# Two cross-attentions with refills by the bank, and a last layer whose heads go by pairs

## What is computed

```python
# third block, cross-attention (l2x): 16 query heads and 4 key heads of 128, 128 context rows
q = (h @ Wq + bq).reshape(b, s, 16, 128); k = (ctx @ Wk + bk).reshape(b, se, 4, 128); v = (ctx @ Wv + bv)
q = rmsnorm(q, qn_w); k = rmsnorm(k, kn_w)
x = x + softmax(q @ k.T / sqrt(128) + mask) @ v @ Wo

# fourth block, cross-attention (l3x): self-attention and cross-attention side by side
ln_out = ln(h)                                  # each projection rounds it to fp8 by its own scale
q, k, v = fp8_linear(ln_out, wq | wk | wv);     q, k = ln(q), ln(k)
core = gqa(q, k, v)                             # 64 own keys
qx = ln(fp8_linear(ln_out, wqx));  kx, vx = split(ctx @ w_kv_x);  kx = ln(kx)
xout = gqa(qx, kx, vx)                          # 128 context keys
x = x + fp8_linear(concat(core, xout), wproj)

# fourth block, feed-forward (l3f): latent attention of 16 heads of 16, then 1 + 7 experts of width 128
kv_d, q_d = r @ kv_d_w, r @ q_d_w               # r = rmsnorm(h)
k, q = concat(kv_d @ k_u_w, rope(r @ rope_k_w)), concat(q_d @ q_u_w, rope(q_d @ rope_q_w))
probs = softmax(causal(q @ k.T / sqrt(16)));    out = (probs @ (kv_d @ v_u_w)) @ o_w
h = h + out;  x = x + h + moe(rmsnorm(h))
```

## Time and profile before

| | |
|---|---|
| median of 3 runs | 3697.68 us (3693.32 to 3700.13) |
| the profiled execution | 3693.92 us, span 3692.1 us |
| TensorE busy in the span | 2963.2 us (80%) |
| VectorE | 2257.9 us (61%) |
| ScalarE | 1502.9 us (41%) |
| GpSimd | 585.9 us (16%) |
| first cross-attention of the change (l2x) | 1608.5 to 1956.0 |
| second (l3x) | 2331.0 to 3008.0 |
| last layer (l3f) | 3371.0 to 3692.0 |

### The profile page before, as it was taken

The page is one execution under the profiler, slowest core; times in us unless marked ns, Lnnn a source line. Parts: engine busy times, 40 slices in busy tenths (PEclk is TensorE's granted clock), DMA queues, the critical chain, the costliest instruction groups (busy, mean ns, idle before and its releaser), DMA issues. The chain is left out here.

```text
span 3692.1 us, 63817 instructions
## 1 busy us (share of the span) xinstructions
PE 2963.2 (80%) x24004; PEld 2073.1 (56%) x24004; DVE 2257.9 (61%) x4830; ACT 1502.9 (41%) x3074; POOL 585.9 (16%) x931
## 2 busy tenths in 40 slices
PE   7777799887868777559987588788888878787878
PEld 3333488776645545325654345355555557666767
DVE  6999544334668888766566523477777654444353
ACT  4889411112446455334431122354554522223332
...
GB/s 125 198 205 205 186 0 0 0 23 9 39 24 3 2 2 2 71 6 6 9 6 70 95 65 0 3 4 6 3 3 3 3 139 1 2 1 1 1 1 12
DMA packets 316540, 141.83 MB, mean 38 GB/s; under 512 B 296221, under 2 KB 305950, under 8 KB 312613
## 3 DMA queue, kind: packets, MB, share of 16 engines
...
## 5 line engine op out<-in xcount | busy, mean ns | idle before, releaser
L1247 ACT ACTIVATE l0x_pb<-l0x_ex,l0x_neg_max,l0x_q_scale 128x2048 uint16<-128x2048 f32 x128 | 267.2, 2088 | 35.1 <-POOL l0x_neg_max L1350 23.5
L1146 PE MATMUL l0x_s_ps<-l0x_kT,l0x_qT 128*128 128x512 bf16 x512 | 178.3, 440 | 76.5 <-DVE l0x_ex L1445 41.1
L1443 DVE TENSOR_SCALAR_CACHE_REDUCE l0x_ex<-l0x_s_ps 128x1024 f32<-128x1024 f32 x128 | 156.2, 1220 | 14.3 <-PE l0x_s_ps L1146 13.3
L1445 DVE TENSOR_SCALAR_CACHE_REDUCE l0x_ex<-l0x_s_ps 128x1024 f32<-128x1024 f32 x128 | 156.1, 1220 | 0.0
L264 PE MATMUL l3x_bank<-l3x_w_kv_x,l3x_ctxT 128*128 128x512 f32 x256 | 127.4, 644 | 24.7 <-ACT l3x_ctx_k L763 14.4
L1146 PEld LDWEIGHTS l0x_s_ps<-l0x_kT,l0x_qT 128*128 128x128 bf16 x512 | 33.4, 101 | 155.8 <-DVE l0x_ex L1445 105.8
L2225 PEld LDWEIGHTS l1a_bank<-l1a_u,l1a_gm 64*64 64x64 f32 x2048 | 95.3, 193 | 17.8 <-issue 17.1
L1156 PEld LDWEIGHTS l0x_o_ps<-l0x_v,l0x_vT 128*128 128x128 f16 x2048 | 71.2, 99 | 60.6 <-DMA l0x_vT<-l0x_pb 31.6
L2225 PE MATMUL l1a_bank<-l1a_u,l1a_gm 64*64 64x8 f32 x2048 | 98.0, 234 | 7.7 <-DVE l1a_gm L2578 7.7
L264 PE MATMUL l2f_bank<-l2f_w,l2f_ln_yT 128*128 128x352 f32 x256 | 103.6, 539 | 0.0
L2217 PE MATMUL l1a_bank<-l1a_r,l1a_r 32*64 32x64 f32 x2048 | 71.0, 279 | 39.8 <-DVE l1a_r L2559 35.6
(11 more groups left out here) (756 smaller groups left out, 7845.8 us busy)
## 6 DMA issues: line engine op xcount, KB each, us to landing
...
l0x_vT<-l0x_pb SPq DMA_TRANSPOSE x128, 4.7
...
```

What stands on the lines that cost most here:

```text
L1146: ins = mm(s_ps[:, j * 512:(j + 1) * 512], qT[:, h, :], kT[:, h // 2, j * 512:(j + 1) * 512], start=True, stop=True)
L1247: s.activation(pb[:, h % 4, :], ex[:, h % 4, :], ACT.Exp, scale=q_scale[:, h:h + 1], bias=nb[:, h:h + 1], accum_out=sums[:, h:h + 1]).then ...
L1443: v.tensor_scalar(ex[:, h % 4, 0:1024], s_ps[:, 0:1024], 1.0, None, ALU.mult, ALU.max, accum_out=low_max[:, h:h + 1]).then_inc(o.up(scores ...
L1445: v.tensor_scalar(ex[:, h % 4, 1024:2048], s_ps[:, 1024:2048], 1.0, None, ALU.mult, ALU.max, accum_out=high_max[:, h:h + 1]).then_inc(o.up ...
```

## The change

Four things change, in three layers.

In both cross-attentions `fill` may take the phase that held its banks, and then waits before each bank for the take of that bank alone. `free` for both banks stays where another user follows; in the loop of l2x, where the four fills get the new arguments too, `free(vp, t)` moves behind `kk.turn` and the wait for the probabilities.

In l2x the bias is split in columns: first those of the keys (512), then the first half of the queries' (1024), then, behind the statistics of the keys, the second half. Each split has four operations in place of seven on the whole, whose two scalars for each row, `below`, are (0, -1, -1) and (0, 0, -1). TensorE waits for one, two and three of them.

In l3x the multiplication back into `xq` becomes a function of its own, which VectorE runs between the two takes of the own heads' output.

In l3f exp works in place on `e` (the clearing at L4533 is of `vv`, 128x512 for each tile, instead of `pb`); two heads of 64 keys are transposed at a time; the values are projected so that both sequences of a pair lie in halves of the partitions, with zeros beside them in `vv` ([P, 2, 8, 32]); the mix has the values as weights (32 columns) and the probabilities as the streamed side, so that the output comes out transposed; further matmuls with `same_head` (a block of ones for each of the two heads) give the denominators in the same layout, repeated over each head's 16 partitions. VectorE takes the reciprocal of 128x256 and multiplies into `outT`.

```diff
-    def fill(self, pe, t):
+    def fill(self, pe, t, freed=None, at=None):
         for u in range(2):
+            if freed is not None:
+                pe.wait_ge(freed.ready.sem, freed.ready.value(at, u + 1))
             self.fills[u](self.banks[u]).then_inc(self.filled.sem, 1)
...
-            pe.wait_ge(bias_split.sem, bias_split.value())
+            pe.wait_ge(bias_split.sem, bias_split.value(0, 1))
             pe.wait_ge(ctx_loaded.sem, ctx_loaded.value(0))
             kk.fill(pe, 0)
             pe.wait_ge(norm.ready.sem, norm.ready.value(0))
+            pe.wait_ge(bias_split.sem, bias_split.value(0, 2))
             q0.fill(pe, 0)
             kk.turn(pe, 0)
-            free(kk, 0)
-            q1.fill(pe, 0)
+            pe.wait_ge(bias_split.sem, bias_split.value(0, 3))
+            q1.fill(pe, 0, kk, 0)
             q0.turn(pe, 0)
-            free(q0, 0)
-            vp.fill(pe, 0)
+            vp.fill(pe, 0, q0, 0)
             q1.turn(pe, 0)
...
-            hi, mid, lo = bias_part
-            pick = env.ident[0:3, 0:3]
             v.memset(ones[:], 1.0).then_inc(s.up(), 1)
-            v.tensor_copy(hi[:], bias[:]).then_inc(s.up(), 1)
-            dve.wait_ge(s.sem, s.at())
-            v.tensor_tensor(bias_rest[:], bias[:], hi[:], ALU.subtract).then_inc(s.up(), 1)
-            dve.wait_ge(s.sem, s.at())
-            v.tensor_copy(mid[:], bias_rest[:]).then_inc(s.up(), 1)
-            dve.wait_ge(s.sem, s.at())
-            v.tensor_tensor(lo[:], bias_rest[:], mid[:], ALU.subtract).then_inc(s.up(), 1)
-            v.tensor_scalar(bias_rows[:], hi[:], pick[:, 0:1], None, ALU.mult).then_inc(s.up(), 1)
-            for n, part in ((1, mid), (2, lo)):
+            v.tensor_scalar(below[:, 0:1], env.ident[0:3, 0:1], -1.0, None, ALU.add).then_inc(s.up(), 1)
+            v.tensor_scalar(below[:, 1:2], env.ident[0:3, 2:3], -1.0, None, ALU.mult).then_inc(s.up(), 1)
+
+            def split_bias(lo, hi):
+                c = slice(lo * P, hi * P)
+                v.tensor_copy(bias_part[:, c], bias[:, c]).then_inc(s.up(), 1)
                 dve.wait_ge(s.sem, s.at())
-                v.scalar_tensor_tensor(out=bias_rows[:], in0=part[:], scalar=pick[:, n:n + 1], in1=bias_rows[:], op0=ALU.mult, op1=ALU.add).then_inc(s.up(bias_split if n == 2 else None), 1)
-            for phase in (kk, q0, q1):
+                v.scalar_tensor_tensor(out=bias_rest[:, c], in0=bias_part[:, c], scalar=below[:, 0:1], in1=bias[:, c], op0=ALU.mult, op1=ALU.add).then_inc(s.up(), 1)
+                dve.wait_ge(s.sem, s.at())
+                v.tensor_copy(bias_part[:, c], bias_rest[:, c]).then_inc(s.up(), 1)
+                dve.wait_ge(s.sem, s.at())
+                v.scalar_tensor_tensor(out=bias_rows[:, c], in0=bias_part[:, c], scalar=below[:, 1:2], in1=bias_rest[:, c], op0=ALU.mult, op1=ALU.add).then_inc(s.up(bias_split), 1)
+
+            split_bias(H, NB)
+            split_bias(0, H // 2)
+            kk.stats_of(first)
+            split_bias(H // 2, H)
+            for phase in (q0, q1):
...
             def begin(t):
-                free(sq1, t)
-                x0.fill(pe, t)
+                x0.fill(pe, t, sq1, t)
                 pe.wait_ge(cross.out_taken.sem, cross.out_taken.value(t, 0))
                 own.score(pe, t)
-                free(sv, t)
-                x1.fill(pe, t)
+                x1.fill(pe, t, sv, t)
 
             begin(0)
...
                 x0.turn(pe, t)
-                free(x0, t)
                 pe.wait_ge(ctx_loaded.sem, ctx_loaded.value(t))
-                kc0.fill(pe, t)
+                kc0.fill(pe, t, x0, t)
...
-                free(x1, t)
-                kc1.fill(pe, t)
+                kc1.fill(pe, t, x1, t)
                 own.mix(pe, t, 0)
                 kc0.turn(pe, t)
 
-                free(kc0, t)
-                vc0.fill(pe, t)
+                vc0.fill(pe, t, kc0, t)
                 own.mix(pe, t, 1)
                 kc1.turn(pe, t)
 
+                vc1.fill(pe, t, kc1, t)
                 free(kc1, t)
-                vc1.fill(pe, t)
                 pe.wait_ge(own.out_taken.sem, own.out_taken.value(t))
                 cross.score(pe, t, 0)
                 part_of_y(t, 0)
 
-                free(vc0, t)
                 if more:
                     pe.wait_ge(xq_ready.sem, xq_ready.value(t + 1))
-                    sk.fill(pe, t + 1)
+                    sk.fill(pe, t + 1, vc0, t)
                 cross.score(pe, t, 1)
                 part_of_y(t, 1).then_inc(own_y_ps.sem, 1)
 
+                if more:
+                    sq0.fill(pe, t + 1, vc1, t)
...
+            def rescale_inputs(o):
+
                 for j, c in parts:
                     v.tensor_scalar(xq[:, j, c, :], xb[:, j, c, :], in_scale[:, j, c:c + 1], None, ALU.mult).then_inc(o.up(xq_ready if (j, c) == parts[-1] else None), 1)
...
                 own.take_out(o, 0)
+                if more:
+                    o.t = t + 1
+                    rescale_inputs(o)
+                    o.t = t
                 own.take_out(o, 1)
...
                     for i in range(4):
-                        ins = nc.tensor.transpose(bank[n % 2][:, i * P:(i + 1) * P], pb[:, 4 * n + i, :], env.ident[:])
+                        u = 8 * n + 2 * i
+                        ins = nc.tensor.transpose(bank[n][:, i * P:(i + 1) * P], e[:, u:u + 2, :].rearrange("p u k -> p (u k)"), env.ident[:])
                     ins.then_inc(pT_ps.sem, 1)
...
                 pe.wait_ge(qk_ready.sem, qk_ready.value(t, 1))
-                mm(first[:, 0:D], lat[:], v_lat[:], start=True, stop=True).then_inc(heads_ps.sem, 1)
+                pe.sem_inc(order["pe"], 1)
+                for b in range(2):
+                    for n, r in enumerate(rows_of):
+                        own_heads = v_lat[:].rearrange("p (i n d) -> p n i d", n=2, d=HD)[:, n, :, :]
+                        ins = mm(first[r, b * P:(b + 1) * P], lat[:, b * S:(b + 1) * S], own_heads, start=True, stop=True)
+                ins.then_inc(heads_ps.sem, 1)
                 yield
...
                 yield from steps(2)
                 pe.wait_ge(exped.sem, exped.value(t))
-                for n in (0, 1):
+                for n in range(2):
                     turn(n)
                 yield
-                for n in (2, 3):
-                    pe.wait_ge(pT_ready.sem, pT_ready.value(t, n - 1))
-                    turn(n)
-                yield
-                for n in (3, 4):
-                    pe.wait_ge(pT_ready.sem, pT_ready.value(t, n))
-                for i in range(H):
-                    ins = mm(first[:, i * HV:(i + 1) * HV], pt[:, i, :], vv[:, i, :], start=True, stop=True)
-                ins.then_inc(out_ps.sem, 1)
-                yield
-                pe.wait_ge(out_ready.sem, out_ready.value(t))
+                pe.wait_ge(pT_ready.sem, pT_ready.value(t))
+                pe.sem_inc(order["pe"], 1)
                 for c in range(DC):
-                    ins = nc.tensor.transpose(other[:, c * P:(c + 1) * P], out[:, 8 * c:8 * c + 8, :].rearrange("p h d -> p (h d)"), env.ident[:])
+                    for b in range(2):
+                        for i in range(4):
+                            mm(first[32 * i:32 * i + 32, c * P + b * S:c * P + (b + 1) * S], vv[:, b, 4 * c + i, :], pt[:, 4 * c + i, b * S:(b + 1) * S], start=True, stop=True)
+                    for i in range(4):
+                        ins = mm(first[32 * i:32 * i + 32, D + c * P:D + (c + 1) * P], same_head[:], pt[:, 4 * c + i, :], start=True, stop=True)
                 ins.then_inc(out_ps.sem, 1)
                 yield
                 pe.wait_ge(outT_ready.sem, outT_ready.value(t))
...
                 act.wait_ge(heads_ps.sem, heads_ps.value(t, VALUES))
-                s.activation(vv[:, :, 0:HD], first[:, 0:D].rearrange("p (h d) -> p h d", d=HD), ACT.Copy).then_inc(o.up(lat_v_ready), 1)
+                for n, r in enumerate(rows_of):
+                    s.activation(vv[r, :, :, n * HD:(n + 1) * HD], first[r, 0:D].rearrange("p (b i d) -> p b i d", b=2, d=HD), ACT.Copy).then_inc(o.up(lat_v_ready), 1)
                 yield from steps(2)
                 act.wait_ge(shifted.sem, shifted.value(t))
-                for b in range(2):
-                    r = slice(b * S, (b + 1) * S)
-                    s.activation(pb[r, :, r], e[r], ACT.Exp).then_inc(o.up(exped if b else None), 1)
+                s.activation(flat(e[:]), flat(e[:]), ACT.Exp).then_inc(o.up(exped), 1)
                 yield
                 take_turned(0)
                 take_turned(1)
-                yield
-                take_turned(2)
-                take_turned(3)
                 yield from steps(2)
-                act.wait_ge(out_ps.sem, out_ps.value(t, TURNED))
-                s.activation(flat(outT[:]), other[:, 0:D], ACT.Copy).then_inc(o.up(outT_ready), 1)
-                yield
                 yield from rms.scalar(o, other, scale=ln2_w, k=2)
...
```

(12 more changed lines are left out.)

72 lines of the change are left out of this document (35 added, 37 removed).

## The result

The changed kernel takes 3598.60 us (median of 4 runs, 3597.89 to 3602.04), the kernel before 3695.72 (4 runs, 3693.32 to 3700.13): a ratio of 0.9738, 95% interval 0.9721 to 0.9755. The direction was right.

A forecast was written before the change was run, and what follows sets the result against it. TensorE's idle time was to be won in the cross-attentions, slow full-width mix matmuls in the last layer. Savings of 40, 19 and 13.7 us sum to 72.7, from 3696.3 to 3624 us; range 3604 to 3652.

The forecast's parts named there:

- -2.3 us a tile: Second cross-attention: moved scaling starts statistics 1.6 us earlier, and a refill no longer awaiting the second take gains 0.7.
- sum -19 us: Second cross-attention: six tiles of 2.3 us (13.8), plus first tile, last tile and prologue; bounds -5 and -27.
- short waits of refills: Second cross-attention: TensorE's idle part read as refills waiting for ScalarE's takes, ctx_k 10.4 us and ctx_q 7.8.
- the refill at 2479.06: Second cross-attention, within a tile: this refill gains 0.75 us itself, which the same chain would give anyway.
- The second rival: Second cross-attention: time a refill gains is waited out at the next take; -5 stays of -19, 3638 us; 10%.
- The cover of the moved scaling: Second cross-attention: scaling between the two head takes ends 0.7 us before the second mix; uncovered, up to 1.66 us a tile.
- Last layer, -40: Last layer's attention: two rounds, each 20.2 us shorter, with VectorE's reciprocals becoming the bound; bounds -38 and -45.
- the first mix: Last layer: a round's first mix starts 6.0 us earlier and takes 2.8 us at the low clock.
- The first rival: Last layer: narrow weight loads and streams don't overlap, 4.9 to 9.8 us a tile; time 3646 to 3685; 14%.
- First cross-attention, -13.7: First cross-attention: keys' bias ready 12.8 us earlier, refill behind the keys gains 0.9; bounds -11 and -14.5.
- The rival on the slower side: Expert stretch behind the last layer's attention: clock stays low, 44.35 us of TensorE work doubles; 3713 us; 2%.
- The rival on the faster side: Second cross-attention's clock doesn't dip and the last layer's mix runs at the high one: -28 and -45; 3610 us; 8%.

The follow-up runs named there:

- e2: The kernel before with only the first cross-attention's change (bias in parts and finer waits): 3662.75 us, ratio 0.9915 to before.
- e6: The changed kernel with each refill waiting for both takes again, in both cross-attentions: 3607.35 us.
- e7: The changed kernel with the eight scalings back ahead of the statistics of kc1: 3621.15 us.
- e11: The changed kernel with the bias split in one go as before and seven one-element writes keeping later code in place: 3608.37 us, ratio 0.9769 to before.

## Why the prediction was wrong in size, step by step

**Second cross-attention, "-2.3 us a tile", "sum -19 us".** With the code in the same good place the order is worth 2.27 us a tile and 20.0 us in the layer, 20.9 of it idle time less 0.9 more busy, so this sum held. What failed is the step before it, in the reading of the trace: the prediction took the period of 79.3 us, and the wait of the transposes L922 for VectorE's probabilities, as given by the work, and put the loading of code at nothing. Some 1.8 us of each tile ahead of those probabilities were waits for code (0.84 and 0.99), and 18.2 us of the layer hung on them. It also called the idle part "short waits of refills": these are 18.2 us in six tiles, and the transposes' wait for scaled rows, 30.0 us, wasn't read. The bounds went to -27 because they counted the waits of refills alone. The edits as such were followed everywhere; that seven instructions in one layer move the code of another was not thought of. The order of instructions that the change brings doesn't tell it, the idle of VectorE with no releaser and the queue of instruction transfers do, and both stood in the trace of before.

**The shares within the 2.3 us** (1.6 for the moved scaling, 0.7 for the finer waits) were wrong, and that their sum was right is partly luck. By e2, e6 and e7 the scaling alone gives 2.12 us a tile and the finer waits alone lose 0.52; on top of the other, the waits give 0.15 and the scaling 2.79. Each of these steps also moved the clock, of which the prediction had nothing. The sentence that the refill at 2479.06 gains 0.75 "which the same chain would give anyway" is the half that was seen: the later refill hangs on the same chain too. The second rival (the finer waits don't do what they say) was right about the tiles for the waits, and by another way: a granted clock that falls with them, not ScalarE. The cover of the moved scaling held: VectorE waited 0.73 us for the second mix behind it.

**Last layer, -40.** Measured -43.1, -21.5 a round, inside the bounds of -38 and -45. The mechanism was right in each link: exp 1.06, first mix 3.0 us behind the begin of the last exp (forecast 3.1), reciprocals of 1.75 us (forecast 1.75), VectorE the bound. The term that was too large is the first mix: 1.7 us at the low clock where 2.8 was forecast, since four groups run side by side and not two. (The 51 ns among its signs should be the 58 of its working; 35 were measured.) The first rival (narrow matmuls that don't overlap), given 14%, didn't come. The rule of the Trainium skill that stood for it, "TensorE: Matmul & The Clock Gate", section "The mechanism", by which a load overlaps a matmul only with another row group, does not hold for these matmuls: all use the same 128 rows, and in the 1.70 us of the window at the low clock loads are under way for 1.65 and matmuls for 1.70. For the reciprocal the two rows of before were better than the estimate from the Trainium skill, "VectorE: DVE Perf Modes", section "First, the fixed hardware budget": 1750 ns, not 2130.

**First cross-attention, -13.7.** Measured -13.8 at the first scores and -14.2 in the whole. Here too the shares differ a little (e11: split 11.4, waits 2.4, forecast 12.8 and 0.9), and in the steady tiles the finer waits gave about 1.5 us where nothing was forecast (3.9 in e6 less 2.4).

**The rival on the slower side** (the clock stays low in the experts) did not come: in the stretch of the experts TensorE works 44.30 of 49.00 us at 0.99, as in the earlier trace rows.

```profile
3408.00:3457.00 49.00, 44.30 (x208) 36.96 (x208) 14.14 (x43) 15.84 (x61) 1.50 (x5) 0.99 0.00 1
```

**The rival on the faster side** (no dips of the clock, 3610) came nearest in the number, not in its cause: the mix begins at the low clock, the granted clock in the second cross-attention is 0.96 after 0.95, and the layer gained 38.2 us against the rival's 28.

**Range and sum.** 72.7 forecast, 18.2 for the place of the code, 3 for the last layer, 1 for the order and 2 in an untouched layer, which varies by more than that between kernels, make the 97. The range was built from the costs of the edits alone. A sum that misses a cause has no bound in it for that cause.
